# Attention in a two-FFN block: the values product moved to one place and a step's work put in another order

## The reference

```
x = x + 0.5 * ffn(layernorm(x))      # 16 experts, top 1, capacity 320, d_ff 512, gelu
x = x + attn(layernorm(x))
x = x + 0.5 * ffn(layernorm(x))

# attn: 8 query heads, 4 key/value heads, head dim 16, rotary positions
q, k, v = x @ Wq, x @ Wk, x @ Wv ; rope(q), rope(k)
scores = q.k * 0.25 + head_scales * (q[:3].dirs) * (k[:3].dirs)
allowed = (j <= i) & ((j < 4) | (j >= i - 127))        # window of 128 and 4 sink keys
out = softmax(where(allowed, scores, -inf)) @ v @ Wo
```

## Time and profile before

| | |
|---|---|
| time, median of 3 runs | 581.42 us (581.08 to 582.9) |
| the profiled execution's own time | 581.05 us |
| its span in the profile | 579.2 us |
| first stage, to the end of its experts | up to about 170 us |
| attention stage | about 170 to 470 us |
| second layer's experts | about 470 us to the end |
| one sequence of attention in full flow | 35.68 us |
| granted TensorE clock, mean | 0.95 |

### The profile page before, as it was taken

One profiled execution on the slowest core, in us unless ns is written; L12 is line 12 of the kernel. 1 busy time (PEld: TensorE's weight loads), 2 busy tenths in 40 slices (PEclk: granted clock), 3 DMA queues, 4 the chain that ended last, 5 costly groups with the idle time before them and its releaser, 6 DMA issues.

```text
span 579.2 us, 10982 instructions
## 1 busy us (share of the span) xinstructions
PE 470.0 (81%) x3044; PEld 309.5 (53%) x3044; DVE 348.1 (60%) x1848; ACT 321.8 (56%) x651; POOL 222.4 (38%) x270
## 2 busy tenths in 40 slices
PE   4454599999184879899998998989899866999990
PEld 3343377777033555555565555656565433777770
DVE  5665224342159777978979789788866562333320
ACT  5354144444144586786877868777786641444430
POOL 3777205455535050500515226152121451054555
PEclk9999999999686699999999999999999986999996
DMA  8831245655236000000000000000000112455540
GB/s 288 268 126 52 63 135 163 178 162 160 84 91 226 1 1 1 20 1 2 19 8 22 16 6 29 11 24 11 29 10 7 43 44 64 138 155 176 152 127 31
DMA packets 44697, 45.54 MB, mean 79 GB/s; under 512 B 4919, under 2 KB 34128, under 8 KB 44616
## 3 DMA queue, kind: packets, MB, share of 16 engines
q1 hardware_dynamic: 40040, 36.74, 21.0%
q0 software_dynamic: 4608, 8.22, 4.2%
HBM read 29.22 MB, written 19.17 MB: 84 GB/s over the span
## 4 chain that ended last, share of the span: by engine, by line
PE 47%; DVE 25%; issue 9%; ACT 9%; POOL 4%; DMA 3%; SPq 1%; POOLq 0%; ACTq 0%; DVEq 0%
PE sc L607 12%; PE b L617 12%; DVE junk L1273 10%; PE b L776 3%; PE sc L715 2%; POOL slots L1455 2%; ACT qT L1056 2%; PE b L596 2%; PE b L687 2%; ACT xn L900 2%; PE b L631 2%; PE b L562 1%; PE sc L741 1%; PE sc L543 1%; PE sc L744 1%
## 5 line engine op out<-in xcount | busy, mean ns | idle before, releaser
L1273 DVE CUSTOM_DVE_ANT_0 junk<-sc,cht 128x256 bf16<-128x256 f32 (+1 forms) x256 | 82.2, 387 | 10.7 <-PE sc L715 10.1
L951 ACT ACTIVATE hT<-sc 128x320 f32<-128x320 f32 x128 | 56.0, 438 | 39.0 <-PE sc L607 28.0
L1455 POOL DMA_INDIRECT slots<-pay,slot_i x64 | 63.5, 992 | 34.9 <-issue 20.9
L1500 POOL COPY vaug<-vall 128x64 f32<-128x64 f32 x32 | 8.4, 264 | 176.3 <-PE b L783 112.9
L607 PE MATMUL sc<-enT,w1s 128*128 128x320 f32 x256 | 74.0, 433 | 0.8 <-DVE enT L1236 0.4
L617 PE MATMUL b<-hT,w2s 128*128 128x320 f32 x256 | 73.8, 432 | 0.0
L1475 POOL DMA_INDIRECT x<-yrow,ytok x40 | 38.9, 973 | 54.5 <-DVE yrow L1246 44.7
L1475 POOL DMA_INDIRECT out<-yrow,ytok x40 | 38.9, 972 | 54.5 <-DVE yrow L1246 44.8
L776 PE MATMUL b<-probs,vaug 128*32 128x256 f32 x448 | 59.8, 386 | 0.0
L1029 ACT ACTIVATE probs<-sc 128x1024 f32<-128x1024 f32 x48 | 49.1, 1023 | 17.5 <-PE sc L744 17.5
L607 PEld LDWEIGHTS sc<-enT,w1s 128*128 128x128 f32 x256 | 47.5, 190 | 19.8 <-issue 1.7
(11 more groups left out here) (165 smaller groups left out, 942.6 us busy)
## 6 DMA issues: line engine op xcount, KB each, us to landing
w1s<-in_L_ffn_w SPq DMA_DIRECT2D x32, 256.0 KB, 3.0
w2s<-in_L_ffn_w SPq DMA_DIRECT2D x32, 256.0 KB, 2.7
slots<-fresh SPq DMA_DIRECT2D x16, 330.0 KB, 4.7
rows<-slots SPq DMA_DIRECT2D x16, 330.0 KB, 3.3
xall<-in_L_attn_x SPq DMA_DIRECT2D x8, 256.0 KB, 4.0
xall<-x SPq DMA_DIRECT2D x8, 256.0 KB, 2.7
out<-xall SPq DMA_DIRECT2D x8, 256.0 KB, 2.3
slots<-pay,slot_i POOLq DMA_INDIRECT x64, 2.4
```

The lines of the kernel that those rows point to most:

```text
L951: nc.scalar.activation(hT[a][:, f, :], hid[f], ACT.Gelu_apprx_tanh).then_inc(e_gelu, 1)
L1273: ins = v.tensor_tensor_reduce(junk[:, H // 2 * h + i, lo:], sc[h][:, i // G, 2 * P * (i % G) + lo:2 * P * (i % G + 1)], tab16["window"][: ...
L1455: gp.indirect_dma_start(out=slots_d[phase], out_offset=bass.IndirectOffsetOnAxis(ap=slot_i[s][:, t:t + 1], axis=0), in_=pay[s][:, t, :], i ...
```

## The change

- `values` now computes all four heads of a tile together, behind `turned_scores` of half 1. The sinks' product is an instruction of its own, `sink_product`, behind `turn_max`.
- PE's list: `turn_sinks` goes ahead of `sink_scores`, `turned_scores` of half 0 ahead of `turn_sums`, `turn_out` ahead of `r_ranks` and `turn_max`, `a_turn` ahead of `a_project`.
- ACT's list: in steps 2 and 3 the first two `normalise` pieces go ahead of both exponentials (one lay between them); the last two of the attention norm go behind the copy of the maxima, with the sinks' exponentials behind them; `r_exps` and `r_pay` go ahead of `qkv_copy`; `anT` is copied ahead of `r_copy`.
- DVE's list: `maxima` is a call for each half, with `r_shift_of` between them in step 3; the cast to `part2` and the parting in `part1` and `rest` are calls of their own; in step 0 `r_route` and `add` go ahead of `stack`; in step 2 `means` goes ahead of `r_place`.
- POOL's list: `scatter` and `rstds` go ahead of `rope`, and the copy to `vaug` to the end of a step (it was the first).

No transfer, tile, bank or shape is changed.

```diff
-            def values(n, t, h, bb):
-                if h == 0:
-                    pe.wait_ge(v_copied, n + 1)
-                    wait(pe, u_copied, n)
-                pe.wait_ge(st_exp, n * 2 + h + 1)
+            def values(n, t):
+                pe.wait_ge(v_copied, n + 1)
+                wait(pe, u_copied, n)
+                pe.wait_ge(st_exp, n * 2 + 2)
                 first = 0 if t else 1
                 for kb in range(first, 2):
-                    for j in (2 * h, 2 * h + 1):
+                    for j in range(KV):
                         last = mm(b5[2 * HD * j:2 * HD * (j + 1), 0:G * P], vaug[:, t - 1 + kb, j, :],
...
                     if has(c, TILES):
                         scores(c, tc)
-                        if tc:
-                            sink_scores(tc, b)
                     if has(e, TILES) and te:
                         turn_sinks(te, be, b)
+                    if has(c, TILES) and tc:
+                        sink_scores(tc, b)
                     if has(d, TILES):
                         turn_q(d, td, bd, b, t + 2)
+                    if has(k, TILES):
+                        turned_scores(k, t, 0, has(c, TILES))
                     if has(f, TILES):
                         turn_sums(f, b, t - 2)
-                    if has(k, TILES):
-                        turned_scores(k, t, 0, has(c, TILES))
-                    if has(e, TILES):
-                        values(e, te, 0, be)
                     if has(d, TILES):
                         turn_k(d, td, b, t + 2)
                     if has(k, TILES):
                         turned_scores(k, t, 1, has(c, TILES))
+                    if has(e, TILES):
+                        values(e, te)
                     if t == 0 and has(b - 2, B):
                         r_logit(b - 2 + B, b, lambda i: i - 2 + B, bank7, b7)
+                    if has(f, TILES):
+                        turn_out(f, b, t - 2)
                     if t == 2 and has(b - 2, B):
                         r_ranks(b - 2 + B, b, lambda i: i - 2 + B, bank7, b7)
                     if has(c, TILES):
                         turn_max(c, b, t + 1)
-                    if has(f, TILES):
-                        turn_out(f, b, t - 2)
-                    if has(e, TILES):
-                        values(e, te, 1, be)
+                    if has(e, TILES) and te:
+                        sink_product(te, be)
...
+                        q_copy(d, td)
+                    if t == 2 and has(b + 3, B):
+                        a_norm_wait(b + 3)
+                        normalise((b + 3) * TB, an, arstd, anbias, a_xn, (0, 1))
+                    if t == 3 and has(b - 1, B):
+                        r_norm_wait(b - 1 + B)
+                        normalise((b - 1) * TB, xn, rstd[0], nbias, r_xn, (0, 1))
+                    if has(k, TILES):
+                        exps(k, t, 0)
+                    if has(d, TILES):
+                        k_copy(d, td)
+                    if has(k, TILES):
+                        exps(k, t, 1)
...
+                        max_copy(c, tc)
+                    if t == 0 and has(b - 2, B):
+                        r_exps(b - 2 + B)
+                    if t == 3 and has(b + 3, B):
+                        anT_copy(b + 3)
+                    if t == 2 and has(b + 3, B):
+                        normalise((b + 3) * TB, an, arstd, anbias, a_xn, (2, 3))
+                    if has(c, TILES) and tc:
+                        sink_exps(tc, b)
+                    if t == 0 and has(b - 2, B):
+                        r_pay(b - 2)
+                    if t == 3 and has(b - 1, B):
+                        r_copy(b - 1 + B)
                     if t < 2 and has(b + 2, B):
                         qkv_copy(b + 2, t)
...
+                        maxima(c, (t + 1) % TB, 0)
+                    if t == 3 and has(b - 1, B):
+                        r_shift_of(b - 1 + B, 0)
...
+                        maxima(c, (t + 1) % TB, 1)
+                    if has(c, TILES):
+                        split_max(c, (t + 1) % TB, b)
+                    if has(c, TILES) and (t + 1) % TB:
+                        sink_diff(t + 1, b)
                     if has(f, TILES):
                         output(f)
...
+                    if t == 0 and has(b + 1, B):
+                        part_rest(b + 1)
+                    if t == 3 and has(b + 2, B):
+                        part(b + 2)
+                    if t == 0 and has(b - 2, B):
+                        r_route(b - 2 + B, (b - 2) % PAYS, 0, scattered_of(b - 2)[1], b7)
...
                     if has(f, TILES):
                         add(f)
+                    if t == 0 and has(b + 1, B):
+                        stack(b + 1, 0)
```

205 lines of the change are left out of this document (90 added, 115 removed).

## The result

The changed kernel takes 575.83 us (median of 12 runs, 573.77 to 579.65), the kernel before 581.51 (12 runs, 578.64 to 584.89): the ratio is 0.9903, 95% interval 0.9885 to 0.9922, so 5.6 us or 1.0% faster. The forecast was 8.1 us faster, 573.0, with a range of its own from 569 to 578. Runs more than 1.5% above the fastest of the same kernel are left out of every ratio, so a ratio can differ from the quotient of the two medians.

What follows compares the result with a forecast made beforehand. DVE was taken to bound most of a sequence, its waits only 3.3 us, with ACT holding step 3 and PE step 0. Gains 2.4 + 1.4 + 1.3 + 1.5 + 1.5 = 8.1 us from 581.05 gave 573.0, range 569 to 578.

Steps and rivals of the forecast that it cites:

- the price of the product: Values on PE: merging both halves saves about 0.97 us per tile with t > 0, 3.4 us per sequence.
- Steps 1 and 2: 17.25 us of a sequence where DVE never waits: a faster PE gives nothing; `rope` loses 0.1.
- Step 0: PE's chain from logits to next scores: scores 0.6 earlier, but DVE is later, so the step gains 0.5 us.
- Step 3: ACT's chain from exponentials to maxima copy, without a gap: hides PE's 0.97, so the step gains only 0.2 us.
- I count the latter 0.2 late: Step 3 on ACT: sinks' exponentials, and with them `turn_sinks`, `turn_q` and the queries' copy, come 0.2 us late.
- Rope beside `stack`: Step 1, POOL's `rope` starts some 0.3 us earlier beside `stack`'s last copies: loss 0 to 0.8 per sequence, 0.1 taken.
- The clock: Attention stage: forecast wrong as a whole if PE with less to do is granted the lower clock; no size given.
- Sequence 0: No routing beside it, both values of steps 3 and 0 on the chain: 0.7 us each, 1.4 gained.
- Sequence 6: DVE waits 4.3 us in one piece: 0.6 from step 3, 0.6 from step 0, 0.3 from steps 1 and 2; 1.5 gained.
- Hidden anyway: Rival: full sequences give nothing and light ones less, 579.7 to 582.8 us; chance 0.12.
- Whole pieces: Rival: both PE pieces come through, steps 3 and 0 of eight sequences gain 0.97 each, 565.5 us; chance 0.10.
- Slower through POOL's rstds: Rival: in step 3 DVE and ACT wait for POOL's `rstds`, 1.6 us lost per sequence, 583.8 us; chance 0.11.

Runs made afterwards that it cites:

- e1_values_only: Kernel before with only the values product merged into one place, sinks' product its own instruction, all other orders old: 601.44 us, ratio 1.0059 to the kernel before.
- e11_turn_max_first: Changed kernel with `turn_max` ahead of `turn_out` on TensorE again, as before the change: 582.24 us, ratio 0.9974 to the kernel before.
- e9_last_rope_lead: Changed kernel; POOL waits for `stack` before the last `rope` only, ScalarE's step 2 norm pieces behind `k_copy` where no tile k yet: 571.17 us, ratio 0.9821.
- after_again: The changed kernel unaltered, run on another chip: 589.73 us, ratio 0.9912 to the kernel before.
- e0_before: The kernel before, unaltered, one run on the same chip as `after_again`: 593.92 us.
- e4_rope_held: Changed kernel with POOL's copy to `vaug` ahead of `rope` in step 1 again: 594.15 us, ratio 0.9941 to the kernel before.

## Why the prediction was nearly right, and where it was wrong

**The direction and the price of the product: right.** PE busy in a sequence is 29.32 (29.0 forecast), 3.1 us less than before, one group of 16 in 1.07 us in a step. Steps 1 and 2 keep their length (8.42 and 8.83 against 8.40 and 8.85), so a faster PE gives nothing where DVE doesn't wait. Of the 2.6 us per sequence that the merged product alone takes off PE, `e1_values_only` shows 0.13 coming through. One slip in the working changed nothing: VectorE's waits in the sequence are four, not five.

**The sum of an undisturbed sequence: 0.6 forecast, 1.07 measured.** Steps 1, 2, 3, 0 were to be 8.5, 8.85, 8.65, 9.1 and are 8.42, 8.83, 8.07, 9.29. Step 0 is right in kind and too large, 0.5 for 0.29: `lmax` starts 5.70 into the step (I had 5.53), after a wait of 0.6 for the logits, and from there to the next `maxima` it is 3.59 (I had 3.49). The 0.1 for `rope` didn't come. Step 3 was too small, 0.2 for 0.78. ACT in it:

```profile
320.39 0.21 ACT L1040 ACTIVATE psk<-psd 128x32 f32<-128x32 f32 x1
...
321.58 1.01 ACT L1013 COPY qT<-b 96x1024 bf16<-96x1024 bf16 x1
322.49 0.88 ACT L901 ACTIVATE xn<-xall,nbias,rstd 128x128 f32<-128x128 f32 x2
323.27 1.00 ACT L1025 ACTIVATE probs<-sc 128x1024 f32<-128x1024 f32 x1
...
326.61 1.00 ACT L1033 COPY qT<-b 12x1024 bf16<-12x1024 bf16 x1
```

The wait of 0.43 is filled, as forecast. But the term "I count the latter 0.2 late" was wrong in sign: the sinks' exponentials start 0.34 ahead of the step where they were 0.16 ahead, 0.18 early. The copy of the queries, which I had 1.10 into the step, stands at 0.85. Of the 0.54 us by which the copy of the maxima comes sooner than forecast (5.88 into the step, not 6.42), 0.25 are this; 0.12 are that the copy and the norms start closer than their lengths that I added, and 0.17 that the work behind them is shorter than the 3.52 I had. I charged the copy of the maxima for what now stands ahead of `turn_max`, and didn't see that the output's copy, which stands ahead of it on ACT, comes sooner: `e11_turn_max_first` has them 0.08 ahead of the step (360.30 against 360.38), 0.26 later than the changed kernel.

**Rope beside `stack`: the mechanism named, the bound too small.** I priced it 0 to 0.8 in a sequence, from a row beside which a single POOL instruction ran. In the full sequences of the changed kernel it cost nothing, or 0.2 where a copy took 1.0 us. In sequence 5 it held VectorE for 2.4 us, and with the dip of the clock that followed the step was 3.2 us longer. The bound should have been the sum of `rope`'s instructions without a gap, 2.2, with the 0.4 that was left of the scatter ahead of them. I forecast -1.3 for that sequence and +1.4 came; `e9_last_rope_lead` shows -1.5 without the collision (32.73 against 34.22). So the expected gain of sequence 5 was there, and one held copy and the dip behind it took it back.

The Trainium skill, page SBUF — State Buffer, section Who interferes with whom, says of the pair of SBUF ports that DVE and GpSimd share that it is an exclusive lock, that the one who issues first keeps it for its whole instruction while the other blocks fully, and that issue order decides. The two orders of sequence 5 agree: copy first by 0.01 us, 0.18 us; copy behind a running POOL instruction, 2.57 us. Against the page's single instruction the copy here stood through four of POOL's, since there was no gap between them. The custom `maxima` started beside the first rope instruction and took 0.40. I had weighed this rule and taken the value near POOL giving way.

**The lead-in: missing from the sum.** I called the stages around attention untouched and didn't walk the new order through the passes in which a tile is absent. Ahead of sequence 0 that cost 0.8 us in the profiled run and nothing in `after_again` against `e0_before`; its price stays open.

**The clock: named as what would make the forecast wrong, priced at nothing.** It is the largest part taken back. In the profiled run four stretches of 3.4 us stand at the lower level in the attention stage. Step by step against the same steps without a dip they cost 1.1 (sequence 2), 1.1 (sequence 5: 11.63, less 8.10 and the 2.4 of the held copy), 0.1 (the seam of 5 and 6) and 0.8 (sequence 7), some 3.1 us. That is an estimate; a held copy without a dip was not measured in sequence 5.

**The sum.** Forecast 8.1. Full sequences 1 to 4: 2.4 forecast, 3.3 measured with one dip in it, and 4.8 in `after_again` against `e0_before`, which have none there. Sequence 0: 1.4, and 1.3; that they agree is in part luck, since the clock was at its lower level for 5.5 us of it in place of 2.4, and `after_again` against `e0_before` (3.8 and 3.9 us there) gained 2.5. Sequence 5: 1.3, and -1.4. Sequence 6: 1.5, and 2.5, since VectorE's waits for the projection shrank from 5.3 to 3.2. Sequence 7 and behind: 1.5, and 1.3, with a dip in its first step. Lead-in: 0, and -2.1, 1.3 of it outside the change. The errors of both signs partly cancelled. With the collision and the lead-in mended, the kernel gains 1.8%, 10.4 us of 582.57: more than forecast, with one dip of the clock in the attention stage in place of four.

**The rivals.** *Hidden anyway* is what the merged product alone is; it is false for the whole change. *Whole pieces* is false: ACT and DVE yield a third of PE's 3.1 us. *Slower through POOL's rstds*: DVE has no wait for it, and the undisturbed step 3 is the part that gained most.

## What to carry to other kernels

Time freed on an engine that the others hide is worth nothing until the order spends it, and an order that spends it costs time without it: test the two together and apart. Where POOL runs several instructions without a gap beside a chain of bf16 copies on DVE, price the collision by the whole series, not by one instruction, and place POOL's series by a wait; but only where the collision happens, since the same wait everywhere gave no gain that could be told. Walk a new order through the first and last passes as well, and compare kernels with the granted clock beside the time: two orders of the same work (the changed kernel and `e11_turn_max_first`, on different chips) were granted 0.935 and 0.922 in the mean, and most of what lay between their ratios went with that.

## What the runs showed of the hardware

- A bf16 copy of 128x128 on DVE, 0.20 us alone, took 2.57 us when it was issued beside a POOL instruction that three more followed without a gap, and ended in a gap of 0.08 us. Issued 0.01 us ahead of POOL's, it took 0.18. Issued beside a scatter behind which POOL left a gap of 0.13 us, it took 0.44 and ended with the scatter.
- Such a held copy cost a full sequence 1.1 us of the 2.3 by which its step grew (`e4_rope_held`, sequence 4, at the upper clock); the next step made up the rest.
- 16 values instructions in four column tiles take 1.07 us where 8 in two take 1.06, also in the middle of a step.
- The program with 10% less PE work per sequence was granted a lower clock (mean of an execution 0.929 to 0.938 over 12 runs, the profiled one of before 0.950), with stretches of 3.4 us at the lower level in the attention stage where the kernel before had none; with the merged product alone it was 0.910 to 0.931. Six matmuls laid into a wait ahead of the dips, or 16 spread over the sequence (1.1 of the 3.1 us given back), didn't bring it back.
- A stretch of 3.4 us at the lower level cost 1.07 us in a full sequence, 0.8 in a first step of sequence 7 and 0.1 across the seam of sequences 5 and 6.
